# Attention in a four-layer network: value products two key tiles behind their scores, split between the head pairs

## The reference, cut to what matters

```python
q, k, v = split(x @ w_qkv.T + b_qkv)            # 16 heads of 16
q, k = rope(q), rope(k)
s = where(causal, q @ k.T / sqrt(16), -inf)     # 1024 x 1024 for each head
y = softmax(s) @ v
```

## Time and profile before

| what | value |
|---|---|
| median of 3 runs | 5204.0 us (5202.71 to 5205.69) |
| the profiled execution's own time | 5199.68 us |
| its span, first to last instruction | 5197.9 us |
| mean granted clock of TensorE | 0.885 of 2.4 GHz |
| PE busy in the span | 3998.3 us (77%) |
| ACT busy | 1889.1 us (36%) |
| DVE busy | 2748.2 us (53%) |

### The profile page before, as it was taken

How to read it: one execution, slowest core, us unless ns; L and a number is a source line. 1 busy time by engine, 2 the same in 40 slices (tenths; PEclk the granted TensorE clock), 3 DMA queues, 4 the chain that set the end, 5 groups by cost and what they waited for, 6 DMA issues and landing times. The chain is left out here.

```text
span 5197.9 us, 56899 instructions
## 1 busy us (share of the span) xinstructions
PE 3998.3 (77%) x20640; PEld 2097.8 (40%) x20640; DVE 2748.2 (53%) x5400; ACT 1889.1 (36%) x2762; POOL 511.6 (10%) x521
## 2 busy tenths in 40 slices
PE   6969869879727869686847677677877886887787
PEld 4515425345212625344335565563324333333332
DVE  5837747558464343434344644646535544544552
ACT  3162261451616364554512332323054035116106
POOL 1000010010010000000000220221201211110120
PEclk9989989889858989898978898898988998998898
DMA  2000000000030000000010000000000000000000
GB/s 80 1 2 1 1 1 1 1 1 1 1 110 1 1 1 1 1 1 1 1 47 1 0 0 0 0 10 33 1 1 9 1 1 9 1 1 9 1 1 9
DMA packets 44768, 44.57 MB, mean 9 GB/s; under 512 B 10320, under 2 KB 40784, under 8 KB 44496
## 3 DMA queue, kind: packets, MB, share of 16 engines
q1 hardware_dynamic: 37424, 31.89, 2.0%
q10 hardware_dynamic: 7072, 9.05, 0.5%
HBM read 36.22 MB, written 4.19 MB: 8 GB/s over the span
## 5 line engine op out<-in xcount | busy, mean ns | idle before, releaser
L572 DVE TENSOR_REDUCE arena<-ps 128x2 f32<-128x1024 f32 (+3 forms) x768 | 725.5, 956 | 329.1 <-PE ps L540 326.9
L698 DVE TENSOR_TENSOR arena<-arena,tri 128x256 f32<-128x256 f32 x512 | 214.9, 425 | 553.1 <-ACT arena L681 449.3
L681 ACT ACTIVATE arena<-ps 128x768 f32<-128x768 f32 (+3 forms) x512 | 408.0, 868 | 116.5 <-PE ps L635 115.6
L652 PE MATMUL ps<-arena 128*17 128x512 f32 (+3 forms) x3072 | 352.0, 566 | 42.3 <-DVE arena L698 42.3
L635 PE MATMUL ps<-arena 64*128 64x512 f16 (+3 forms) x1536 | 220.3, 369 | 191.1 <-ACT arena L681 170.5
L1739 ACT ACTIVATE arena<-ps 128x512 f32<-128x512 f32 x96 | 52.5, 594 | 797.2 <-PE ps L1680 751.6
L1170 PE MATMUL ps<-arena 128*128 128x512 f32 x576 | 311.3, 629 | 0.0
L1186 ACT ACTIVATE arena<-ps 128x512 f32<-128x512 f32 x144 | 86.0, 597 | 618.4 <-PE ps L1170 618.4
L652 PE MATMUL ps<-attention 128*33 128x512 f32 (+3 forms) x1536 | 302.7, 503 | 0.0
L698 DVE TENSOR_TENSOR attention<-attention,tri 128x256 f32<-128x256 f32 x256 | 108.8, 425 | 354.2 <-ACT attention L681 238.9
L1155 PE MATMUL ps<-arena 128*128 128x256 f32 x1152 | 292.2, 393 | 0.8 <-DVE arena L1203 0.8
(11 more groups left out here) (267 smaller groups left out, 6671.8 us busy)
## 6 DMA issues: line engine op xcount, KB each, us to landing
making<-basis SPq DMA_DIRECT2D x16, 768.0 KB, 4.4
out<-x_all SPq DMA_DIRECT2D x8, 512.0 KB, 3.0
arena<-w_down SPq DMA_DIRECT2D x1, 2304.0 KB, 24.7
x_all<-x SPq DMA_DIRECT2D x2, 1024.0 KB, 14.2
x_all<-x ACTq DMA_DIRECT2D x2, 1024.0 KB, 19.9
arena<-arena SPq DMA_DIRECT2D x128, 4.0 KB
making<-w_gate_up SPq DMA_DIRECT2D x1, 2048.0 KB, 15.2
arena<-w_qkv SPq DMA_DIRECT2D x2, 768.0 KB, 6.0
```

The source lines that it names most:

```text
L572: dve.reduce_max(a.mp[:, 2 * j:2 * j + 2, qt, c], out[:, :, 0:w], AX.X).then_inc(self.pair_out, 1)
L652: last = pe.matmul(m.ps[width * hh:width * hh + w, c, q0 - c * CH:CH], a.v[:, kt, vh, :], p, start=(kt == 0), stop=(kt == TC * (c + 1) - 1))
L681: act.activation(a.p[:, u + odd, kt * P:S], m.ps[:, b:b + 2, :].rearrange("p a b -> p (a b)")[:, kt * P:S], ACT.Exp, scale=HD ** -0.5).the ...
L698: dve.tensor_tensor(diag, diag, keep, ALU.min).then_inc(masked, 1)
```

## The change

In `attention`, `lag` is 2 for every call. TensorE's order within a step becomes: score of pair 0, chunk 0 of `values(n - 2)` (or its only chunk), score of pair 1, the rest of `values(n - 2)`. The wait for `masked` stands before the first chunk, `summed` still rises after chunk 1. The last two steps' products follow in the same loop. With `maps` = 2 (the second layer) `lag` was 2 already and both chunks follow the only pair's score, so that call's order stays as it was. The first and fourth layer's ring has 10 rows where it had 8, so pair v takes the rows of pair v - 5.

```diff
@@ -597,7 +597,7 @@
     groups, pairs = NM // maps, maps // 2
     n_pair = pairs * groups * NT
     ring = a.p.shape[1]
-    lag = 1 if maps == 4 else 2
+    lag = 2
@@ -637,10 +637,11 @@
-            def values(n):
+            def values(n, chunks):
                 g, kt = divmod(n, NT)
-                pe.wait_ge(masked, pairs * (n + 1))
-                for c in range(kt // TC, NC):
+                if chunks:
+                    pe.wait_ge(masked, pairs * (n + 1))
+                for c in chunks:
                     if kt == 0 and g >= 1:
                         pe.wait_ge(evac, NC * (g - 1) + c + 1)
@@ -651,15 +652,15 @@
-                last.then_inc(summed, 1)
-
-            for n in range(groups * NT):
+                    if c == NC - 1:
+                        last.then_inc(summed, 1)
+
+            for n in range(groups * NT + lag):
+                chunks = range((n - lag) % NT // TC, NC) if n >= lag else range(0)
                 for j in range(pairs):
-                    score(pairs * n + j)
-                if n >= lag:
-                    values(n - lag)
-            for n in range(groups * NT - lag, groups * NT):
-                values(n)
+                    if n < groups * NT:
+                        score(pairs * n + j)
+                    values(n - lag, chunks if pairs == 1 else chunks[:1] if j == 0 else chunks[1:])
@@ -1892,7 +1893,7 @@   (first layer; the same at L2036, fourth layer)
-            a = attention_memory(m, ar, NM, HD, NM // 4, 8)
+            a = attention_memory(m, ar, NM, HD, NM // 4, 10)
```

## The result

| | before | changed |
|---|---|---|
| median of 20 runs each | 5199.75 us | 5210.31 us |
| ratio of the changed kernel to the one before | | 1.0019, interval 1.0012 to 1.0026 |
| profiled execution, span | 5197.9 us | 5208.5 us |
| mean granted clock over the span | 0.885 | 0.878 |

The change costs some 10 us, about the 0.2% that I had set as the bound of "no change"; the interval lies clear of 1, so the kernel did get slower. Forecast were 20 us in the other direction. One of the 20 runs of before took 5437 us, far from all the others, and has no part in the ratio.

What follows compares the result with a forecast made beforehand. The prediction took ScalarE's chain of exponents to bound the stage. Removing old gaps (-141 us) and adding new waits (+121 us) gave -20 us from the 5204 median: 5184 us, range 5156 to 5214.

Steps and rivals of the forecast that it cites:

- The bound: Attention executions of the changed call: ScalarE leads, busy some 76 us of 94.2 to 97.4; gains are read from its gaps.
- The old gaps at tiles 4 and 7: ScalarE's gaps of 14.3 and 17.4 us there, put at zero; with tiles 2 and 3, 141 us including overlap.
- the mask waits: TensorE's 42.3 us of idle time waiting for masks before products, forecast to fall below 15.
- The new wait: Second pair's exponent waits for a chunk to free its row, tiles 2 to 5; 70 us at full clock.
- the chain: Steps from the first pair's first exponent to the second pair's; added waits 0.99 us at tile 2, 1.00 at tile 3.
- the low clock's term: Extra on the new waits where tiles meet the low clock, 32 x 1.17 h; all new waits then 121 us.
- h: Mean number of tiles per group whose chain meets the low clock: tile 2 always, tile 3 one in three; taken as 1.35.
- the surcharge at tile 2: Low clock's extra per tile met: 0.85 us on a chunk plus 0.32 on scores, 1.17 us.
- The wait only changed its name: Rival: score-queue wait returns as free-row wait, same tile and size; h 1.6 to 2.2, 5204 +- 10, 24 in 100.
- My range up to 5214: Forecast range 5156 to 5214 us, including the case without a change and most of the little-low-clock case.
- The slower rival: TensorE and ScalarE take turns, low clock lasts over tiles 2, 3 and half the next; +23 us, 5227, 14 in 100.
- the break-even at h = 1.89: Value of h at which new waits equal the old gaps: (4.40 - 2.19) / 1.17.

Runs made afterwards that it cites:

- fill10: Changed kernel (lag 2, split, ten rows) plus idle products after each pair's scores of key tiles 0 and 1; 5131.8 us, 0.987 of the kernel before.
- fill_before: Kernel before (lag 1, whole products, eight rows) plus idle products, three chunks per group, at tiles 0 and 1; 5128.3 us, 0.986 of the kernel before.
- lag2_whole12: Changed kernel with products whole behind the second pair's scores and 12 rows; 5192.4 us, 0.998 of the kernel before.

## Why the prediction was wrong

- **The bound, and where the gaps are: right.** From the first exponent to the last store the eight executions grew from 753.7 to 762.7 us, 8.9 of the 10.6 us by which the span grew, and ScalarE's busy time in them did not grow. That tile 2's gap would stay near 75 us and tile 3's come to about 40 was too low: 85.2 and 52.8.
- **The old gaps at tiles 4 and 7 go, the mask waits fall below 15: right** (1.4, 0.0 and 4.1 us).
- **The new wait, its place and its mechanism: right.** Products release the 768- and 640-element exponents. At full clock the chain gave 0.99 and 1.00 us beyond a back-to-back start, 0.11 of which is overlap and not idle time; `fill10` has 0.96 and 1.01 idle, so 1.07 and 1.12.
- **The step that failed is the low clock's term, 32 x 1.17 h with h = 1.35.** The new waits, this term in them, were to cost 3.77 us per group. Tile 2 costs 84.4 / 32 + 0.11 = 2.75 where my terms give 0.99 + 1.17 = 2.16; tile 3 costs 50.9 / 32 + 0.11 = 1.70 where they give 1.00 + 0.35 x 1.17 = 1.41. Together 0.88 us per group, 28 us of the 30 between the forecast of -20 and the measured +10.
- **Why the surcharge at tile 2 was too small.** I doubled chunk 1 and the second pair's scores and left chunk 0 out, since at full clock it is hidden behind the first pair's exponent. At the low clock it isn't: its products start at 301.29 and last 1.91 us, the exponent from 301.65 ends near 302.46, and the scores that could have followed it start at 303.13. That is 0.67 us of delay where my chain has 0.06, so 0.61 too little, and 0.59 is what was missing in all.
- **Why h was too small.** Counted through the timelines of all 32 groups, tile 2 met the low clock in every one, and tile 3 waited for 1.0 us in 14 and for 2.0 to 2.2 us in 18. I had said one in three; it was 18 in 32, so h was 1.56. With that alone the forecast would have been -12 us: the sign hung on the surcharge at tile 2.
- **What I had credited to the order.** I subtracted old gaps as the trace had them, the low clock in them, from new waits mostly priced at the full clock. Like with like, at full clock, the old gaps at tiles 2, 3, 4 and 7 are 15.5 + 15.5 + 14.3 + 17.4 = 63 us (`fill_before`) and the new ones at tiles 2 to 5 are 30.8 + 32.4 + 1.4 + 4.4 = 69 (`fill10`). At full clock there was nothing to gain with ten rows. The prediction never priced its old gaps at the full clock.
- **The rivals.** The wait only changed its name: 5204 +- 10 holds the 5210, and what released the exponents is as that rival says. Its number is in part luck: it asked for h from 1.6 to 2.2 and for gaps of the same size, and h was 1.56 while the gap at tile 3 grew from 20.5 to 52.8. My range up to 5214 holds the 5210 only because it took in the case without a change. The slower rival named the other half, a clock that stays low over tile 3, but the break-even at h = 1.89 was set too high by the small surcharge. The rule of the Trainium skill that I weighed ("TensorE: Matmul & The Clock Gate", part 1, the HAM clock gate), a low clock by default that activity lifts, is what `fill10` used: the granted clock went from 0.80 to 1.00 in the first execution when TensorE was given more to do, so this trace agrees. I gave it too little weight.

The cause is shown on both sides: more rows remove the new wait, a filled lull removes its excess. Left open is what sets how long the clock stays low in a group; no run here varied that finely.

## What to carry to other kernels

When work is moved to a later step and a buffer rotates, write out for each writer which reader it waits for and where that reader's signal now stands in its queue. Here ten rows in place of twelve turned a gain of 73 us into a loss of 10. Price old and new waits at the same clock; an old gap that holds a low clock is not saved by reordering if the low clock moves along, as it did in `lag2_whole12`. And where TensorE has a lull ahead of work on the critical chain, products nobody reads can be cheaper than the pause: 72 us here for 96 extra chunks, 78 for 128, and no memory.

## What the runs showed of the hardware

Half of the idle products held the clock almost as well as all of them: 5085.9 against 5084.6 us, with one stretch at the low clock in the first execution (the row 277.00:283.60 above). And the low clock cost nearly the same in two quite different orders, 72 and 78 us, although the mean granted clock of their executions differs (0.82 to 0.86 before, 0.78 to 0.84 changed). So the mean clock alone does not give the price here; that it depends on which chunks the low clock falls on fits the timelines, but no run varied it by itself.
